# Edge softmax of a graph network on one Trainium2 core: two groups of a block in one VectorE instruction, and per-group marks read at register addresses

## What is computed

```python
w_m = (efeat @ W_msg + b_msg).reshape(E, 16, 16)
w_a = (efeat @ W_attn + b_attn).reshape(E, 16, 16)
h_src = feat[src][:, :, None]
e1, e2 = w_m * h_src, w_a * h_src
seg_max = segment_max(e2, dst)
ex = exp(e2 - seg_max[dst])
attn = ex / segment_sum(ex, dst)[dst]
ft = segment_sum(e1 * attn, dst).sum(axis=1)
```

## Time and profile before

| | us |
|---|---|
| median of 3 runs (lowest 3267.5, highest 3271.28) | 3270.18 |
| the profiled execution | 3269.55 |
| its span, first to last instruction | 3267.7 |
| VectorE busy over the span | 2494.0 |
| TensorE busy over the span | 2426.8 |
| ScalarE busy over the span | 1861.9 |
| mean granted TensorE clock | 0.700 |

### The profile page before, as it was taken

How to read it: one execution, slowest core, us unless ns; L and a number is a source line. 1 busy time by engine, 2 the same in 40 slices (tenths; PEclk the granted TensorE clock), 3 DMA queues, 4 the chain that set the end, 5 groups by cost and what they waited for, 6 DMA issues and landing times. The chain is left out here.

```text
span 3267.7 us, 39524 instructions
## 1 busy us (share of the span) xinstructions
PE 2426.8 (74%) x7146; PEld 911.0 (28%) x7146; DVE 2494.0 (76%) x4298; ACT 1861.9 (57%) x7322; POOL 1358.8 (42%) x1220
## 2 busy tenths in 40 slices
PE   0888887785982689975688888888887888788740
PEld 0111111133551445533222222222222222222210
DVE  5999999943012445411699999999999999999977
ACT  2888888700000111110788788788878877887820
POOL 3000000006664400002676666666666766666503
PEclk8555556677975799987566766676677667667665
DMA  1000000002332554420122222222222222222113
GB/s 16 0 0 0 0 0 0 0 3 78 89 85 73 144 182 147 143 79 18 30 65 74 64 69 77 65 69 71 71 65 65 77 65 69 77 65 69 56 61 86
DMA packets 122244, 201.37 MB, mean 62 GB/s; under 512 B 55143, under 2 KB 76536, under 8 KB 116320
## 3 DMA queue, kind: packets, MB, share of 16 engines
q1 hardware_dynamic: 84192, 170.52, 15.0%
q0 software_dynamic: 38016, 30.45, 5.4%
HBM read 72.73 MB, written 128.17 MB: 61 GB/s over the span
## 5 line engine op out<-in xcount | busy, mean ns | idle before, releaser
L1463 POOL DMA_INDIRECT hs<-h_table,gix x880 | 1064.3, 1209 | 492.8 <-issue 265.7
L1555 ACT ACTIVATE e<-wps,hs 128x32 f32<-128x32 f32 x5632 | 1009.9, 590 | 201.1 <-PE wps L1487 160.0
L1487 PE MATMUL wps<-w_edge,ef 18*128 18x512 f32 x1760 | 729.7, 895 | 336.9 <-DVE e L1593 187.4
L1509 PE MATMUL slot_sums<-e,ident 128*128 128x512 f32 x1056 | 572.6, 700 | 9.7 <-DVE e L1658 9.7
L357 PE MATMUL acc<-q_hot,lo_hot 128*128 128x400 bf16 x1200 | 469.0, 495 | 132.8 <-DVE q_hot L327 70.3
L1487 PEld LDWEIGHTS wps<-w_edge,ef 18*128 18x128 f32 x1760 | 217.9, 248 | 812.9 <-DVE e L1593 337.2
L311 ACT ACTIVATE lo_hot<-lane,loT 128x128 bf16<-128x128 f32 x1200 | 353.7, 387 | 19.4 <-PE acc L357 19.2
L336 DVE TENSOR_TENSOR edges<-acc,edges 128x400 f32 x600 | 338.5, 564 | 22.6 <-PE acc L357 17.0
L1509 PEld LDWEIGHTS slot_sums<-e,ident 128*128 128x128 f32 x1056 | 230.6, 227 | 377.8 <-issue 367.3
L1593 DVE TENSOR_TENSOR e<-wps,hs 128x1024 f32<-128x1024 f32 (+1 forms) x220 | 314.6, 1430 | 26.9 <-PE wps L1487 26.9
L327 DVE TENSOR_SCALAR q_hot<-qcol,qT 128x400 bf16<-128x400 bf16 x1200 | 325.9, 313 | 5.3 <-issue 4.1
(11 more groups left out here) (305 smaller groups left out, 1979.8 us busy)
## 6 DMA issues: line engine op xcount, KB each, us to landing
rows_state<-states SPq DMA_DIRECT2D x44, 1280.0 KB, 4.6
rows_shift<-shifts SPq DMA_DIRECT2D x44, 640.0 KB, 3.0
edges_order<-got SPq DMA_DIRECT2D x56, 256.0 KB, 2.6
got_order<-edges_order SPq DMA_DIRECT2D x56, 256.0 KB, 2.9
ef_order<-efT SPq DMA_DIRECT2D x56, 256.0 KB, 3.0
hs<-h_table,gix POOLq DMA_INDIRECT x880
ef<-ef_order SPq DMA_DIRECT2D x44, 320.0 KB, 3.0
msg<-m_parts SPq DMA_DIRECT2D x10, 480.0 KB, 4.9
```

The lines of the kernel that those rows point to most:

```text
L1463: nc.gpsimd.indirect_dma_start(out=hs[u][:, s, :], out_offset=None, in_=d["h_table"], in_offset=bass.IndirectOffsetOnAxis(ap=gix[u][:, s:s ...
L1487: nc.tensor.matmul(wps[:, bank, :], ef[u][k:k + KM, g * P:(g + 1) * P], w[k:k + KM, :], start=True, stop=True).then_inc(a_mult, 1)
L1509: ins = nc.tensor.matmul(sums[:, (u + g) % 2, :], ident[:, :], e[u][:, g * SLOTS + c, :], start=(c == 0), stop=(c == SLOTS - 1))
L1555: ins = nc.scalar.mul(e[u][:, s, at], wps[:, bank, at], hs[u][:, s, f:f + 1])
```

## The change

Groups 3 and 4, whose slots VectorE adds itself, are taken together: one `weigh` of 2048 elements, one `halve` of 2048 and one `quarter` of 1024 in place of two each. The single `halve` stands where the one of group 3 stood; the single `quarter` stands where the one of group 3 stood, behind `up` of group 0, with the wait for `a_halved`. The copy of the marks is dropped: `up`, `down`, `rescale` and `accumulate` read their mark from the whole table, at an address that in the loop depends on the register b.

```diff
-    NM = 2
...
-        mk = [sb(f"mk{u}", [P, BG, NM]) for u in range(2)]
...
-                def masks(v, u, b):
-                    v.add(nc.vector.tensor_copy(mk[u][:, :, :], marks[:, cols(b, BG), :]))
+                def mark(b, g, which):
+
+                    at = b * BG + g
+                    return marks[:, at, which:which + 1] if isinstance(b, int) else \
+                        marks[:, bass.ds(at, 1), which:which + 1].rearrange("p a n -> p (a n)")
...
-                def up(v, u, g):
+                def up(v, u, b, g):

                     before = shift(u, g - 1) if g else shift(1 - u, BG - 1)
-                    return v.add(nc.vector.scalar_tensor_tensor(shift(u, g), before, mk[u][:, g, 0:1], shift(u, g),
+                    return v.add(nc.vector.scalar_tensor_tensor(shift(u, g), before, mark(b, g, 0), shift(u, g),
                                                                 ALU.add, ALU.max))

-                def down(u, g):
+                def down(u, b, g):

                     return nc.vector.scalar_tensor_tensor(
-                        shift(u, g - 1), shift(u, g), mk[u][:, g, 0:1], shift(u, g - 1), ALU.add, ALU.max)
+                        shift(u, g - 1), shift(u, g), mark(b, g, 0), shift(u, g - 1), ALU.add, ALU.max)
...
-                def rescale(u):
+                def rescale(u, b):

                     nc.vector.scalar_tensor_tensor(
-                        scale[u][:, :].rearrange("p (i o) -> p i o", o=F), shift(1 - u, BG - 1), mk[u][:, 0, 0:1],
+                        scale[u][:, :].rearrange("p (i o) -> p i o", o=F), shift(1 - u, BG - 1), mark(b, 0, 0),
                         shift(u, 0), ALU.add, ALU.subtract).then_inc(a_sub, 1)
...
-                def group(u, g):
-                    return e[u][:, g * SLOTS:(g + 1) * SLOTS, :].rearrange("p c n -> p (c n)")
+                own = [e[u][:, BYPE * SLOTS:BLK, :].rearrange("p (g c) n -> p g (c n)", c=SLOTS) for u in range(2)]

                 def weigh(v, u, b):

                     dve.wait_ge(a_exp, (b + 1) * (BG + 1))
-                    for g in range(BG):
-                        pair = e[u][:, g * SLOTS:(g + 1) * SLOTS, :].rearrange("p c (i a o) -> p (c i) a o", a=2, o=F)
+                    for g0, g1 in (*((g, g + 1) for g in range(BYPE)), (BYPE, BG)):
+                        pair = e[u][:, g0 * SLOTS:g1 * SLOTS, :].rearrange("p c (i a o) -> p (c i) a o", a=2, o=F)
                         ins = nc.vector.tensor_tensor(pair[:, :, 1, :], pair[:, :, 0, :], pair[:, :, 1, :], ALU.mult)
-                        if g < BYPE:
+                        if g0 < BYPE:
                             ins.then_inc(a_weighed, 1)
                         else:
                             v.add(ins)

-                def halve(u, g):
-
-                    both = group(u, g)
-                    return nc.vector.tensor_tensor(both[:, 0:HALF], both[:, 0:HALF], both[:, HALF:2 * HALF], ALU.add)
-
-                def quarter(v, u, g):
-
-                    both = group(u, g)
-                    v.add(nc.vector.tensor_tensor(both[:, 0:HALF // 2], both[:, 0:HALF // 2],
-                                                  both[:, HALF // 2:HALF], ALU.add))
+                def halve(u):
+
+                    return nc.vector.tensor_tensor(own[u][:, :, 0:HALF], own[u][:, :, 0:HALF],
+                                                   own[u][:, :, HALF:2 * HALF], ALU.add)
+
+                def quarter(v, u):
+
+                    v.add(nc.vector.tensor_tensor(own[u][:, :, 0:HALF // 2], own[u][:, :, 0:HALF // 2],
+                                                  own[u][:, :, HALF // 2:HALF], ALU.add))
...
                         ins = nc.vector.scalar_tensor_tensor(states[u][:, g, :], states[u][:, g - 1, :],
-                                                             mk[u][:, g, 1:2], total, ALU.mult, ALU.add)
+                                                             mark(b, g, 1), total, ALU.mult, ALU.add)
...
                     weigh(v, w, b - 1)
                     v.wait(v.n)
-                    v.add(halve(w, 3))
+                    halve(w).then_inc(a_halved, 1)
                     carry(v, w, b - 1, i * 16 + 16 * u)
-                    masks(v, u, b)
-                    halve(w, 4).then_inc(a_halved, 1)
...
                     v.wait(found)
-                    shifted = up(v, u, 0)
-                    quarter(v, w, 3)
+                    shifted = up(v, u, b, 0)
+                    dve.wait_ge(a_halved, b + 1)
+                    quarter(v, w)
                     v.wait(shifted)
-                    shifted = up(v, u, 1)
+                    shifted = up(v, u, b, 1)
                     accumulate(v, w, b - 1, 0)
                     v.wait(shifted)
                     for g in range(2, BG):
-                        v.wait(up(v, u, g))
+                        v.wait(up(v, u, b, g))
                     downs(v, u, b)
-                    rescale(u)
+                    rescale(u, b)
...
                     next_block(1)
-                    dve.wait_ge(a_halved, b + 1)
-                    quarter(v, w, 4)
                     next_block(2)
...
                 v.wait(v.n)
-                for g in range(BYPE, BG):
-                    v.then(halve(1, g))
-                    quarter(v, 1, g)
+                v.then(halve(1))
+                quarter(v, 1)
                 v.wait(v.n)
```

More of the change, by code:

```diff
@@ L1617, in largest @@
                         pairs[:, g0:g1, 0:F, :], pairs[:, g0:g1, F:2 * F, :], ALU.max))
-                def up(v, u, g):
+                def up(v, u, b, g):
                     before = shift(u, g - 1) if g else shift(1 - u, BG - 1)
-                    return v.add(nc.vector.scalar_tensor_tensor(shift(u, g), before, mk[u][:, g, 0:1], shift(u, g),
+                    return v.add(nc.vector.scalar_tensor_tensor(shift(u, g), before, mark(b, g, 0), shift(u, g),
                                                                 ALU.add, ALU.max))
-                def down(u, g):
+                def down(u, b, g):
                     return nc.vector.scalar_tensor_tensor(
-                        shift(u, g - 1), shift(u, g), mk[u][:, g, 0:1], shift(u, g - 1), ALU.add, ALU.max)
+                        shift(u, g - 1), shift(u, g), mark(b, g, 0), shift(u, g - 1), ALU.add, ALU.max)
                 def downs(v, u, b):
                     for g in (4, 3, 2):
-                        v.then(down(u, g))
-                    down(u, 1).then_inc(a_shift, 1)
+                        v.then(down(u, b, g))
+                    down(u, b, 1).then_inc(a_shift, 1)
                     dve.wait_ge(a_shift, b + 1)
@@ L1707, in _ @@
                 v.add(nc.vector.memset(shifts[1][:, BG - 1, :], 0.0))
-                masks(v, 0, 0)
                 dve.wait_ge(a_gather[0], GM)
@@ L1717, in _ @@
                 for g in range(BG):
-                    v.wait(up(v, 0, g))
+                    v.wait(up(v, 0, 0, g))
                 downs(v, 0, 0)
-                rescale(0)
+                rescale(0, 0)
                 for g in reversed(range(BG)):
```

## The result

The kernel with the change takes 3306.55 us (median of 5 runs, 3305.01 to 3308.11); the kernel before, with two further runs beside it, 3271.28 (5 runs, 3267.5 to 3275.73). The ratio is 1.0107, with a 95% interval of 1.0092 to 1.0122: **slower by 35 us**, where 29.9 were forecast and 3284 to 3316 was the range. The profiled execution took 3305.47 us, 35.9 above that of before.

What follows compares the result with a forecast made beforehand. VectorE, busy 391.09 of 400 us, and ScalarE's nearly closed second loop bound it. Part A 18.20 plus part B 18.19 made a block 36.39 us, up 0.73: 29.2 us in 40 blocks plus 0.7, so 3300 us, range 3284 to 3316.

Steps and rivals of the forecast that it cites:

- Part A: From the maximum of groups 3 and 4 to the end of group 0's subtraction: 17.29 us, growing to 18.20.
- part B: From the end of group 0's subtraction to the next maximum of groups 3 and 4: 18.19 us, by ScalarE.
- The quarter: Merged and all at the first place: part A grows by 0.535 us, part B's VectorE work falls by 0.60.
- The addresses: Up pass, groups 0, 3 and 4: three bare register instructions at 0.125 us each, 0.375 us in part A.
- A (free): Register addresses cost nothing, since the queue runs ahead: 15 us slower, 3285 us; chance 0.15.
- B (dearer): Addresses not used again in down pass and rescale: 25 us more, 3325; or 0.165 each, 3305; chance 0.1.
- ScalarE's floor: ScalarE's 96 late-slot instructions, a fixed 17.15 us, keep part B from falling below 18.19 us.
- C: ScalarE's late slots shrink and the addresses are free: faster by 12 us, 3258 us; chance 0.05.
- D: ScalarE gives way but the addresses are bare: block 35.75 us, 4 us slower, 3274 us; chance 0.05.
- Rival E: TensorE's late products at a low clock make ScalarE wait 0.35 us: 14 us on the forecast, 3314; chance 0.05.
- The small savings: In part B: weigh 0.07, halve 0.07, mark copy 0.08, quarter 0.60 us; all together worth only 0.18 us.
- the slack: Before the maximum of groups 3 and 4, kernel before: ScalarE would have let it start 0.18 us earlier.

Runs made afterwards that it cites:

- fresh kernel: The kernel with the change, with the same mark addresses written another way in down pass and rescale so they are made anew: 3325.63 us, ratio 1.0163.
- the disturbed set: A set of follow-up runs in which ScalarE had idle time with no releaser the profile shows; the kernel before took 3370.82 us there.
- e3: The kernel before with only weigh and halve of groups 3 and 4 merged: 3270.06 us, ratio 0.9986.
- e5: The kernel with the change, with the up pass's five addresses made at the head of the block, before any wait: 3289.82 us, ratio 1.0053.
- e9: e8 with slots 14 and 15 ahead of 12 and 13 on TensorE and ScalarE: 3255.95 us, ratio 0.9953 to the kernel before.
- e1: The kernel with the change, with the quarter of group 4 back in part B: 3283.2 us, ratio 1.0025.
- e2: The kernel with the change, with the marks copied again and read at constant addresses: 3294.28 us, ratio 1.0062.
- e4: The kernel before with only the mark copy dropped and marks read at register addresses: 3284.73 us, ratio 1.003.
- e6: The kernel with the change, with down pass and rescale addresses written another way so they are made anew: 3325.63 us, ratio 1.0163.
- e7: The kernel before with the quarter of group 4 moved behind product 2, where VectorE waits for TensorE: 3265.47 us, ratio 0.998.
- e8: The kernel before with weigh, halve, quarter merged, quarter behind product 1, accumulation 3 behind product 2, late slots 18, 19 before 12 to 15: 3371.37 us, ratio 0.9995.

## Why the prediction was right, and what was off

**The two parts of the block** were right: this is why the time went up while VectorE's work went down. Part A measured 2443.38 - 2425.14 = 18.24 us (forecast 18.20), part B 18.26 (forecast 18.19). The wait for ScalarE, forecast as 0.64 us, is 0.63 in the view. From start to start it is 0.72, since the view counts from the recorded end of the instruction ahead, and without a wait the next one starts about 0.08 us before that end. VectorE's own count is so 36.50 - 0.72 = 35.78, forecast 35.75.

**The quarter** put 0.53 us into part A (2427.65 to 2428.78, 1.13, for 0.60), as said. It also had a small companion that was not forecast: the `up` right behind it lasts 0.52 instead of 0.48, and the next instruction starts 0.05 later. With the copy back, at a constant address, that step has the same length (0.53), and with the quarters apart, at a register address behind a small quarter, it has the old one (0.48), so this belongs to the larger quarter ahead and not to the address.

**The addresses**: three bare ones, at 0.125 us each, were forecast; measured are 0.13 before group 0 (2426.39 to 2427.24, 0.85, for 0.72) and 0.24 for groups 3 and 4 together. The three terms of part A are so 0.53 + 0.05 + 0.37 = 0.95, forecast 0.91. Reuse in the down pass was right (one row of four, 2.06 us, as before, and no register instruction of its own), and so was the cover of the accumulations' four addresses (0.66 us from such a start to the next, as before). So rivals A (free) and B (dearer) fell; the fresh kernel shows what B would have been, 53 us above the kernel before beside it, where B had 55. Where the two rules of the Trainium skill differed, the runs side with "Vector Engine (DVE) Microarchitecture Reference", Instruction fetch and dispatch: the wait goes ahead of the register instruction. The rule of the Trainium skill, "Advanced Engine Details and Errata", Sequencer Loop, that instructions can be read and queued while the ucode works on a control instruction, frees an address only where no unmet wait hangs on it, as with the addresses made ahead, whose gaps are gone, and with those of the accumulations.

**The term that was mis-sized is ScalarE's floor.** The prediction took 17.15 us for its 96 late instructions, and after they take 17.23, 0.08 us more. Part B as a whole came out 0.07 above its forecast (18.26 for 18.19), 2.9 us in 42 blocks. With the 0.04 of part A, 1.7 us, that is 4.6 of the 4.8 us by which the 42 blocks missed the forecast (34.7 against 29.9). Of the 1.2 us left of the 35.9, 1.1 come from ahead of the changed code. It is not the new order that does it. The ramp is ordered alike in both kernels, and there too the 96 take 17.24 us after, against 17.17:

```profile
1605.14 17.24 ACT L1553 ACTIVATE e<-wps,hs 128x32 f32<-128x32 f32 x96 [6.69 <-PE wps L1485]
```

Apart from the disturbed set, a trace has one of two values in nearly every block: 17.15 (and 5.80 for the 32 early ones) in the kernel before, `e3`, `e5` and `e9`, 17.23 (and 5.82) in the kernel after, `e1`, `e2`, `e4`, `e6` and `e7`. The kernel with fresh addresses has 5.80 in its first profiled execution, of the disturbed set, and 5.82 in its second, on another chip, so it isn't fixed by the kernel's text either; and chips don't sort them, since the kernels with 5.80 and with 5.82 ran on the same ones. What sets it stays open. A comparison of blocks from single profiled executions carries this 0.08 us, 0.1% of the whole, in either direction, wherever ScalarE is the bound; in the step from the kernel before (17.15) to the kernel after (17.23) it is most of what the forecast missed, and not an effect of the change.

**Rivals C and D** needed the 96 instructions to give way. In no trace did they take less than 17.15 us. (The prediction set the mark for C too high: under 16.8 us wins back the 0.355, but C's 3258 needs part B down at 35.375 - 17.825 = 17.55, and so the 96 in about 16.5.) **Rival E** needed TensorE to come late for ScalarE; in all 44 blocks after, the 96 follow each other without a gap, and the mechanism showed itself elsewhere, in `e8`, through the order of TensorE's rows.

**The small savings** of part B (0.07, 0.07, 0.08 and 0.60 us) were worth only the slack, as forecast, and the kernel with `weigh` and `halve` alone shows that they are real where nothing is added to A.

## What to carry to other kernels

When one engine is 98% busy and another 80%, look in the order of time for the second loop: cut the cycle where the two hand over, and add up each part with the slower engine's own chain. Work moved across such a cut costs in full, and what is saved on the other side is worth only the slack. Where an operand's address is in a register, have it made before the wait that the instruction takes; and where an engine waits for small products, see that successive ones in TensorE's queue don't share rows.

## What the runs showed of the hardware

- An address that is made behind a wait of VectorE for itself costs 0.12 to 0.13 us, though its register instructions take 64 to 89 ns in the queue: the gap is 0.16 us instead of 0.035. Made ahead, or used again, it costs nothing that shows.
- An idle time of nothing in the waits view is no sign that an engine isn't waiting: in the kernel with the quarters apart L1614 starts 0.03 us after ScalarE's end in every block, and no idle time is listed.
- ScalarE's 96 small instructions take 17.15 or 17.23 us, one or the other for nearly all blocks of an execution; the 32 early ones take 5.80 or 5.82, and of these the same kernel had both kinds.
- A product behind one on the same rows of TensorE (slot 12 behind 16) was ready 3.82 us after the other's start; on other rows (slot 14 behind 16) 2.59.
- In one set of runs ScalarE stood without instructions for 99.1 us of 1360, and the kernels that ran in this set and in another, the one before too, took 3 to 5% more in this one.
